# The opening of an attention and feed-forward kernel, remade: fewer warming passes, bias rows added inside PSUM, weight parts on VectorE, factor parts on ScalarE

## What is computed

```python
x = x + attn(xn, g, b, w_in, b_in, w_out, b_out) + ffn(xn, W1, b1, W2, b2)

# attn: 16 heads of 16 channels, keys are the queries
z = layernorm(xn) * g + b
q, k, v = split(z @ w_in.T + b_in);  k = q
out = softmax(q @ k.T / 4) @ v;      return out @ w_out.T + b_out
# ffn: 1024 hidden channels, weights rounded to -1, 0 or 1
h = gelu(xn @ ternary(W1).T + b1);   return h @ ternary(W2).T + b2
# ternary(w) = clip(round(w / mean(abs(w))), -1, 1)
```

## Time and profile before

| | us |
|---|---|
| median of 3 runs | 1382.27 (1381.38 to 1382.33) |
| the profiled execution, its own time | 1382.0 |
| its span on the core | 1379.8 |
| busy PE / DVE / ACT / POOL | 1359.6 / 1311.3 / 1244.9 / 230.6 |

### The profile page before, as it was taken

The page is one execution under the profiler, slowest core; times in us unless marked ns, Lnnn a source line. Parts: engine busy times, 40 slices in busy tenths (PEclk is TensorE's granted clock), DMA queues, the critical chain, the costliest instruction groups (busy, mean ns, idle before and its releaser), DMA issues.

```text
span 1379.8 us, 32101 instructions
## 1 busy us (share of the span) xinstructions
PE 1359.6 (99%) x13296; PEld 460.9 (33%) x13296; DVE 1311.3 (95%) x1350; ACT 1244.9 (90%) x2268; POOL 230.6 (17%) x385
## 2 busy tenths in 40 slices
PE   9899999999999999999999999999999999999999
PEld 6566642222222222222222222222222222222244
DVE  7888899999999999999999999999999999999935
ACT  7575569999999999999999999999999999999975
POOL 3212162000000000000000003333200225501200
PEclk9999999999999999999999999999999999999999
DMA  5333300000010001111010111000001112202122
GB/s 226 73 86 72 92 18 24 26 26 30 31 33 33 33 33 33 34 33 33 33 34 33 33 33 36 31 31 31 28 29 40 56 58 66 64 32 65 41 88 101
DMA packets 55724, 66.71 MB, mean 48 GB/s; under 512 B 33329, under 2 KB 38865, under 8 KB 55324
## 3 DMA queue, kind: packets, MB, share of 16 engines
q1 hardware_dynamic: 55146, 63.55, 14.7%
q10 hardware_dynamic: 434, 1.13, 0.2%
HBM read 40.77 MB, written 16.77 MB: 42 GB/s over the span
## 4 chain that ended last, share of the span: by engine, by line
DVE 81%; PE 15%; issue 1%; DMA 1%; ACT 1%; POOL 0%; SPq 0%; DVEq 0%
DVE part_max L988 79%; PE ps L1336 3%; PE ps L1245 3%; PE ps L1265 2%; PE ps L504 2%; PE ps L485 1%; PE ps L383 1%; PE ps L474 1%; DMA max_rows<-max_split 1%; PE ps L1358 0%; DVE w L980 0%; PE ps L514 0%; DMA x_parts<-weight_scratch 0%; PE ps L413 0%; DMA qry<-max_rows 0%
## 5 line engine op out<-in xcount | busy, mean ns | idle before, releaser
L988 DVE TENSOR_REDUCE part_max<-ps 128x1 f32<-128x1024 f32 x1024 | 1160.5, 1295 | 3.4 <-PE ps L383 3.4
L1220 ACT ACTIVATE w<-ps 128x512 f32<-128x512 f32 x2048 | 1109.4, 596 | 51.3 <-PE ps L474 16.3
L413 PE MATMUL ps<-w,v_ones 128*32 128x256 f32 (+1 forms) x7688 | 627.1, 398 | 0.3
L427 PE MATMUL ps<-qry,key 50*128 50x512 f16 x1984 | 398.9, 386 | 8.0 <-ACT w L1220 7.5
L383 PE MATMUL ps<-qry,key 48*128 48x512 f16 x2048 | 393.3, 380 | 0.7 <-DVE part_max L988 0.7
L413 PEld LDWEIGHTS ps<-w,v_ones 128*32 128x32 f32 x7688 | 151.3, 108 | 313.3 <-issue 160.2
L427 PEld LDWEIGHTS ps<-qry,key 50*128 50x128 f16 x1984 | 98.2, 92 | 430.0 <-ACT w L1220 412.3
L751 POOL COPY v_ones<-v_all 128x128 f32<-128x128 f32 x64 | 18.5, 291 | 689.0 <-PE ps L413 689.0
L383 PEld LDWEIGHTS ps<-qry,key 48*128 48x128 f16 x2048 | 100.0, 93 | 76.2 <-issue 16.0
L1336 PE MATMUL ps<-x_parts,w_ternary 128*128 128x512 f16 x256 | 62.0, 380 | 0.9 <-ACT hidden L1177 0.9
L1177 ACT ACTIVATE hidden<-ps,columns 128x512 f32<-128x512 f32 x64 | 41.2, 677 | 20.0 <-PE ps L1336 19.7
(11 more groups left out here) (169 smaller groups left out, 534.3 us busy)
## 6 DMA issues: line engine op xcount, KB each, us to landing
key<-q_parts SPq DMA_DIRECT2D x62, 128.0 KB
qry<-q_parts SPq DMA_DIRECT2D x62, 128.0 KB
o_heads<-o_evacuated SPq DMA_DIRECT2D x31, 256.0 KB, 9.9
key<-q_parts SPq DMA_DIRECT2D x66, 64.0 KB
qry<-q_parts SPq DMA_DIRECT2D x66, 64.0 KB
resid<-in_x SPq DMA_DIRECT2D x8, 512.0 KB, 7.7
q_parts<-q_split SPq DMA_DIRECT2D x16, 256.0 KB, 2.5
out<-resid SPq DMA_DIRECT2D x7, 512.0 KB, 4.0
```

Source lines behind the costliest of these rows:

```text
L413: mm = eng.matmul(pv[32 * c:32 * c + 2 * D, c0:c1], vst[:, kb, :], prob[kb % 2][:, c * BANK + c0:c * BANK + c1], start=(kb == 0), stop=(kb ...
L427: eng.matmul(ring_bank(v, i, False), key[v][r:r + KROWS, kb * P:(kb + 1) * P], qry[v][r:r + KROWS, c * BANK:(c + 1) * BANK], start=True, s ...
L988: dve.tensor_reduce(part_max[h % 2][:, blk, side:side + 1], pa[a % 2], AX.X, ALU.max).then_inc(s_r, 1)
L1220: act.activation(prob[kb % 2][:, c * BANK:(c + 1) * BANK], ring_bank(k, i, last), ACT.Exp, scale=exp_scale).then_inc(s_e, 1)
```

## The change

The lines below are from the diff, cut to its core. `WARM` falls from 16 to 10. The load of group 0's rows is cut in two, and the power -0.5 of group 0 is taken in two instructions. The replicas of the reach are made by ScalarE and not by VectorE. The absolute bias rows are a product of one row that starts each sum in PSUM, and one reduction gives both maxima. The products of `b` with the weights come behind the transposes.

```diff
-WARM = 16
+WARM = 10
 # SyncE
-            load_x(0)
+            sp.dma_start(resid[:, 0:TG // 2, :], x_v[0][:, 0:TG // 2, :]).then_inc(s_x0, 16)
+            sp.dma_start(resid[:, TG // 2:TG, :], x_v[0][:, TG // 2:TG, :]).then_inc(s_x[0], 16)
...
-            sp.wait_ge(s_sg, 8)
+            sp.wait_ge(s_sg, 6)
...
+            x_parts_in(1)
+            factors_in(1)
             store_q(0)
-            x_parts_in(1)
 # GpSimd: rsqrt(0), replicate(1), factor_rows(g)
+                    pool.tensor_tensor(rstd[:, 0, :], veps[:, 0, :], expo[:, 0, :], ALU.pow).then_inc(s_rs, 1)
+                    pool.tensor_tensor(rstd[:, 1, :], veps[:, 1, :], expo[:, 1, :], ALU.pow).then_inc(s_r0, 1)
...
                 if g == 1:
-                    pool.wait_ge(s_ft, 1)
-                else:
-                    pool.wait_ge(s_fx, 16 * (g - 1))
+                    return
+                pool.wait_ge(s_fx, 16 * (g - 1))
...
                 pool.wait_ge(s_qf, KC * g)
+                pool.wait_ge(s_xs, g)
 # VectorE: sigma in part, and its new followers
+                dve.wait_ge(s_qb, 1)
+                dve.tensor_reduce(bound[:, 0:2], pq[0].rearrange("p (s n) -> p s n", s=2), AX.X, ALU.max)
...
+            def wq_first_parts():
+                dve.wait_ge(s_wqv, 16)
+                dve.wait_ge(s_sg, 5)
+                for k in range(KC):
+                    dve.tensor_scalar(wqp[:, 0, k, :], wq[:, k, :], gq_col[:, k:k + 1], None, ALU.mult).then_inc(s_wqs, 1)
+
+            def weight_seconds(w, col, parts, first, done):
+                for k in range(KC):
+                    dve.wait_ge(first, k + 1)
+                    last = dve.scalar_tensor_tensor(out=parts[:, 1, k, :], in0=w[:, k, :], scalar=col[:, k:k + 1], in1=parts[:, 0, k, :],
+                                                    op0=ALU.mult, op1=ALU.subtract)
+                last.then_inc(done, 1)
...
 # ScalarE
+            for k in range(KC):
+                last = act.activation(reach_rep[:, k, :], ones[:, :], ACT.Identity, scale=gabs[:, k:k + 1], bias=babs[:, k:k + 1])
+            last.then_inc(s_rr, 1)
+            act.wait_ge(s_row, 16)
+            act.activation(row_abs[:, :], row[:, 0:2 * C], ACT.Abs).then_inc(s_rb, 1)
...
+            def wv_first_parts():
+                act.wait_ge(s_sg, 6)
                 for k in range(KC):
+                    act.activation(wvp[:, 0, k, :], wv[:, k, :], ACT.Identity, scale=gv_col[:, k:k + 1]).then_inc(s_wvs, 1)
+
+            def factor_parts_of_1():
+                act.wait_ge(s_fb, 2)
+                act.activation(f_rep_parts[:, 0, :, :], f_big[:, :].unsqueeze(2).to_broadcast((P, TG, P)), ACT.Copy).then_inc(s_fb, 1)
+                act.wait_ge(s_fb, 3)
+                for t in range(TG):
+                    last = act.activation(f_rep_parts[:, 1, t, :], f_rep_parts[:, 0, t, :], ACT.Identity, scale=-1.0,
+                                          bias=f_big[:, t:t + 1])
+                last.then_inc(s_fb, 1)
 # TensorE
+                    if first and o:
+                        pe.wait_ge(s_bv, 1)
...
+            pe.wait_ge(s_rr, 1)
+            pe.wait_ge(s_rb, 1)
+            for n, (out, cols) in enumerate(((bound_q, absq), (bound_v, absv))):
+                pe.matmul(out, ones[0:1, :], row_abs[:, n * C:(n + 1) * C], start=True, stop=False)
+                pe.wait_ge(s_abs, n + 2)
                 for k in range(KC):
+                    mm = pe.matmul(out, reach_rep[:, k, :], cols[:, k, :], start=False, stop=(k == KC - 1))
```

More of the change, by code:

```diff
@@ L112, in attention_ffn @@
         babs = sb("b_abs", [P, KC])
-        reach = sb("reach", [P, KC])
         reach_rep = sb("reach_rep", [P, KC, P])
@@ L846, in stats_of @@
                 x = resid[:, g * TG:(g + 1) * TG, :]
-                dve.wait_ge(s_x[g], 16)
+                if g == 0:
+                    dve.wait_ge(s_x0, 16)
+                else:
+                    dve.wait_ge(s_x[g], 16)
                 for t in range(TG):
+                    if g == 0 and t == TG // 2:
+                        dve.wait_ge(s_x[g], 16)
                     last = dve.bn_stats(stats[:, t, :], x[:, t, :])
@@ L912, in add_ffn @@
                                          op0=ALU.mult, op1=ALU.add).then_inc(s_ra, 1)
-            def reach_of_q():
-                dve.wait_ge(s_abs, 1)
-                dve.tensor_tensor(reach[:, :], gabs[:, :], babs[:, :], ALU.add).then_inc(s_sg, 1)
-                dve.wait_ge(s_sg, 1)
-                for k in range(KC):
-                    last = dve.tensor_scalar(reach_rep[:, k, :], ones[:, :], reach[:, k:k + 1], None, ALU.mult)
-                last.then_inc(s_sg, 1)
             def sigma():
@@ L933, in sigma, with other_scales @@
-                dve.tensor_reduce(bound[:, 2:3], vbound_row[:, :], AX.X, ALU.max).then_inc(s_sg, 1)
+                dve.reciprocal(inv2[:, :], floor2[:, :]).then_inc(s_sg, 1)
                 dve.wait_ge(s_sg, 4)
-                dve.tensor_scalar(bound[:, :], bound[:, :], 2.0 ** -40, 2.0 ** 60, ALU.max, ALU.min).then_inc(s_sg, 1)
+                dve.tensor_scalar(gq_col[:, :], g_col, inv2[:, 0:1], TOP, ALU.mult, ALU.mult).then_inc(s_sg, 1)
+            def other_scales():
+                dve.tensor_scalar(unsig[:, :], floor2[:, 0:1], 1.0 / TOP, None, ALU.mult)
+                dve.tensor_scalar(vun[:, :], floor2[:, 1:2], 1.0 / HTOP, None, ALU.mult)
+                dve.tensor_scalar(hu[:, :], floor2[:, 2:3], 1.0 / HTOP, None, ALU.mult)
+                dve.tensor_scalar(gv_col[:, :], g_col, inv2[:, 1:2], HTOP, ALU.mult, ALU.mult)
+                dve.tensor_scalar(vsc[:, :], inv2[:, 1:2], HTOP, None, ALU.mult)
+                dve.tensor_scalar(hs[:, :], inv2[:, 2:3], HTOP, None, ALU.mult)
@@ L1189, in _ @@
             group(0, True)
-            act.wait_ge(s_wvp, 1)
             stage_first(1)
@@ L1193, in _ @@
                 value(0, j)
+            factor_parts_of_1()
             act.wait_ge(s_ob, 1)
@@ L1286, in factor_transposes, with bias_products @@
                 mm.then_inc(s_ft, 1)
+            def bias_products():
+                for out, w in ((b_wq, wq), (b_wv, wv)):
+                    for o in range(KC):
+                        for k in range(KC):
+                            mm = pe.matmul(out[:, o:o + 1], w[:, k, o * P:(o + 1) * P], b_col[:, k:k + 1], start=(k == 0), stop=(k == KC - 1))
+                mm.then_inc(s_qb, 1)
             def group(g, between=None, early=None):
@@ L1358, in _ @@
                 pe.matmul(pf[1][:, 0:P], ones[:, :], ones[:, :], start=True, stop=True)
-            pe.wait_ge(s_row, 16)
-            pe.matmul(bank(3), ones[0:1, :], row[:, 0:2 * C], start=True, stop=True).then_inc(s_rp, 1)
             pe.wait_ge(s_abs, 1)
             pe.matmul(sum_b1, ones[:, :], b1abs[:, KF:KF + 1], start=True, stop=True)
-            pe.wait_ge(s_abs, 2)
-            pe.wait_ge(s_sg, 2)
-            for out, cols in ((bound_q, absq), (bound_v, absv)):
-                for k in range(KC):
-                    mm = pe.matmul(out, reach_rep[:, k, :], cols[:, k, :], start=(k == 0), stop=(k == KC - 1))
-            mm.then_inc(s_qb, 1)
-            for out, w in ((b_wq, wq), (b_wv, wv)):
-                for o in range(KC):
-                    for k in range(KC):
-                        mm = pe.matmul(out[:, o:o + 1], w[:, k, o * P:(o + 1) * P], b_col[:, k:k + 1], start=(k == 0), stop=(k == KC - 1))
+            pe.wait_ge(s_rr, 1)
[3 more added lines that the diff above has]
+                pe.wait_ge(s_abs, n + 2)
+                for k in range(KC):
+                    mm = pe.matmul(out, reach_rep[:, k, :], cols[:, k, :], start=False, stop=(k == KC - 1))
             mm.then_inc(s_qb, 1)
```

87 lines of the change are left out of this document (37 added, 50 removed).

## The result

| | before | after |
|---|---|---|
| median, us | 1381.41 (22 runs) | 1384.43 (22 runs) |
| lowest to highest, us | 1380.91 to 1382.34 | 1381.15 to 1392.1 |
| ratio, 95% interval | | 1.0023 (1.0015 to 1.003) |
| the profiled execution, own time and span | 1382.0, 1379.8 | 1388.76, 1386.6 |

The changed kernel is slower by 0.23%, 3.0 us, outside the range given, and its executions differ by 11 us where those of before differ by 1.4. The profiled one is among its slowest: it lies 4.3 us above the median, so the trace shows an unlucky case and not the typical one.

What follows compares the result with a forecast made beforehand. VectorE's row maxima, untouched, make 79% of the last chain; the change moves only group 1's first gelu. Transpose 3.0 us earlier, group 2's normalising 0.7 to 1.7 later, net 0.6: 1382.0 - 0.6 = 1381.4, median 1381.6; range 1379.5 to 1383.0.

Steps and rivals of the forecast that it cites:

- the price of the missing passes: Opening, TensorE: twelve bounds rows at about 0.43 us in the low clock, ending at 11.1 as before.
- The gap in q of group 0: TensorE stands 0.7 us between q's halves, waiting for the other scales and bias columns; q ends at 20.0.
- rival 1: Opening: clock already up by the bounds; gelu starts 1.6 to 2.6 us earlier, 1380.1 us; chance 0.25.
- VectorE's gain: Group 1 on VectorE: work up to the rows' transpose ends sooner, so the transpose starts 3.0 us earlier than 40.36.
- The two signs by which I would have called the forecast wrong: Groups 1 and 2: rstd of group 2 not waiting for the row sum, or line 998 keeping 1.5 us each.
- TensorE is through at 5.3 us, before the clock had come up: Opening: ten warming passes are 20 rows of 0.21 us from 1.04, ending at 5.3 us, still at the lower clock.
- rival 4: Opening through hidden blocks, TensorE: clock stays low much longer, some 4.5 us lost, 1386 us; chance 0.05.
- half loads ... act before 9 us, where the low clock sets the pace: Opening: half loads and group 0's split power cost nothing.
- a constant shift to the end: After group 1's first gelu: the program is a fixed list, so the 0.6 us shift passes through one to one.
- Rival 3: Group 1: GpSimd's power and VectorE's line 836 exclude each other; everything behind 1.3 us later, 1383.0 us; chance 0.10.
- Rival 2: Group 2: the factors are not late, so the transpose's 3.0 us gain stays, 1379.3 us; chance 0.08.

Runs made afterwards that it cites:

- e2: The changed kernel with 16 warming passes instead of 10: 1381.91 us, ratio 1.0002 to the kernel before.
- e1: The changed kernel with group 0's rows loaded by one DMA again: 1386.9 us, ratio 1.0033 to the kernel before.
- e3: The changed kernel with GpSimd's power (rstd) of group 2 ahead of the row sum of group 1: 1384.1 us, ratio 1.0016 to the kernel before.
- e5: The kernel before with only the warming cut from 16 to 10 passes: 1383.04 us, ratio 1.0014.
- e7: The changed kernel with one whole load of group 0's rows, 16 passes and group 2's power ahead of the row sum: 1378.80 us, ratio 0.9983.
- e8: The changed kernel with 16 passes and group 2's power ahead of the row sum, half loads kept: 1379.41 us, ratio 0.9991.
- e6: The changed kernel with one whole load of group 0's rows and 16 passes, GpSimd's order as changed: 1381.66 us, ratio 0.9999.
- e10: The changed kernel with one whole load and group 2's power ahead of the row sum, ten passes kept: 1381.53 us, ratio 1.0008.
- e11: e7 with the ten other-scale instructions ahead of the first ternary half of w1: 1378.64 us, ratio 0.998 to the kernel before.
- e4: The kernel before with only the load of group 0's rows cut in two: 1381.81 us, ratio 1.0004.
- e12: e8 with the load of w1 written behind ScalarE's first activation, though its issue did not move: 1380.33 us, ratio 0.9986 to the kernel before.
- e9: e8 with the ten other-scale instructions ahead of the threshold of w1: 1379.2 us, ratio 0.9986 to the kernel before.

## Why the prediction was wrong

The step that failed is the price of the missing passes. I charged the low clock for the twelve rows of the bounds alone and found that it changed nothing there. The runs show 2.5 us in the median for the six passes (e2) and a spread of 11 us, and the traces show where: a low clock that lasts past the bounds, to 14 us in e1, 18 in after and 25 in e3, and in after, e1 and e5 a second stretch of it between 45 and 57. The half loads, to which I gave no cost, add to it in the executions in which the weights land late.

**Right: how the work is strung together.** From VectorE's variance on, every step of the working is in the trace with its size, only 5 us later. Line 998 takes 4.87 (4 x 1.24 forecast) and line 905 1.22. The rows' transpose is issued at 42.33 and the row sum starts 5.7 behind it (4.7 to 5.7 forecast). The normalising of group 2 comes 8.55 behind the transpose's issue (7.6 to 8.6 forecast), and the gelu 2.45 behind that (2.56). The gap in q of group 0 is 0.83 us in e2 and e7 (0.7). Where the clock is up and the weights are early, rival 1's times hold too: in e7 the transpose is at 35.93 (35.8 forecast). That GpSimd's order, with the factors' transpose now second in SyncE's queue, takes back most of VectorE's gain is shown by e2 to e8 and e6 to e7: 2.5 and 2.9 us. The two signs by which I would have called the forecast wrong did not appear: rstd of group 2 did wait for the row sum, and line 998 ran at its clean pace. What failed was outside them.

**Wrong, first: "TensorE is through at 5.3 us, before the clock had come up", with the low clock charged up to the bounds alone.** I gave a row 0.43 us at the lower clock and 0.25 at the upper, which put the end of the bounds at 11.1 as before, and took the rest at full speed. A row costs 0.52 us at the lower level, 0.09 more than I had, and the clock does not come back when the sparse part ends: it is at 0.50 from 11 to 17 us after, and it falls again at 50 to 58. Nor did ten passes always leave the clock down: in four of the five profiles with ten passes (after, e3, e5, e10) it was up by the warming's last row or by the first rows behind it, and only in e1 was it still low when the bounds began. In after and e3 it then fell in the wait of 3.80 and 3.57 us for the late weights, in e5 behind one of 0.94, and in e10, with no such wait, it stayed up. In the kernel before the warming reaches to 7.8, past the absolute weights at 6.6 and the replicas of the reach at 7.4, and leaves no wait. That the passes are worth their time because they bridge it is my reading of these traces; no experiment separates it from their work on the clock itself. The low clock is rival 4 in kind, to which I gave 0.05 on the ground of the `KEEP` passes; they run at 20.25 after, too late for the bounds, the transposes and the `b` products. The ten passes cost 2.5, 5.2, 4.7 and 2.7 us in four pairs, and 1.6 in the kernel before (e5).

**Wrong, second: "half loads ... act before 9 us, where the low clock sets the pace", and cost nothing.** I counted the tiles they bring and not what their second issue is put ahead of. With the load in one piece the q and v weights were first read between 5.89 and 6.04 in every profile (before, e1, e5, e6, e7, e10, e11). With halves it was 5.88, 6.67, 7.08, 8.53, 9.28, 9.57 and 9.81 (e8, e2, e4, e12, e9, e3, after). A late landing moves the start and also opens a hole in TensorE, of 2.2 us in e12, 3.0 in e9, 3.6 in e3 and 3.8 in after, in or behind which the clock falls. On the median this is small, 0.3 and 0.6 us with sixteen passes, and with ten the two pairs disagree even in sign; it widens the spread (5.8 against 1.6 us, e8 and e7). In the profiled execution of after, TensorE's first product with the weights starts 3.9 us later than the 6.6 that I had. VectorE reads the bounds at 15.76 (11.1 forecast), and q of group 0 starts at 22.11 (16.5 forecast), 5.6 late. Of the gap of 0.7 between its halves less than 0.2 is left, so q ends 5.1 late (25.1, 20.0 forecast).

**Wrong, third: the place of the new hole.** I said that the emptying of the second bank is queued behind the late normalising, and charged only its lateness. It also leaves TensorE idle for 2.7 to 2.9 us (after, e1, e2, e6), and in three of these four traces (all but e2) the twelve rows behind it run at a lower clock. The forecast of "a constant shift to the end" failed with it: in the profiled execution of after the gelu is 4.8 us late, group 3 and all behind it 5.7, and the end 6.8. The last 1.0 is the longer wait for the row maxima where the heads end.

**The rivals.** Rival 3 did not happen: rstd of group 1 starts at 30.62, line 845 starts at 30.88 inside it and takes its plain 1.29, and the power ends after 1.64. The Trainium skill (SBUF — State Buffer, section "SBUF: two separate sides") says that a GpSimd instruction and a VectorE one in a two-port mode, or one with two inputs in SBUF, exclude each other on their shared ports for a whole instruction. Line 845 takes 1.29 us for as many elements as line 849, with two inputs, handles in 2.34, so I count it as of the first kind, and this pair does not show the rule; line 849 beside GpSimd's small product does (last section). My reading of the 2.92 us in the earlier trace rows, that the power's result could not be written during line 836, is not settled: in before, e4 and e5 the power took 2.92 and ended 0.04 or 0.05 us behind line 836, but in the changed kernel its plain end already lies behind line 845 (32.26 and 32.17 after). Rival 2, that the factors are not late, did not happen either. e7 makes it true by an edit and reads 1378.8, where it was priced at 1379.3, but with the clock up besides, so that the two numbers lie close is no confirmation.

**The starting point.** I subtracted from the median of three runs, 1382.27. With 22 runs the kernel before reads 1381.41, so the forecast time was 0.9 us too high from the start. (1382.27 less 0.6 is also 1381.7, and I wrote 1381.6.) As a change the forecast was 0.7 us down, and 3.0 up was measured.

**The range.** It took the spread of the runs of before, 1 us, for a kernel whose executions differ by 11. Six passes fewer remove the reserve that made every execution alike, and a median of a wide distribution lies above the execution that the steps describe.

**Open.** Why the same hole of 2.8 us lowers the clock in one execution and not in another (e6 and e2). Whether it is the distance between the issue of the q and v weights and that of `w1`, or the cut itself, that makes the landing vary: e12 did not move the issue, and an order with the weights ahead of the second half was not tried. Nor was the factors' transpose put back ahead of the rows', and what the other parts of the change are worth (bias rows in PSUM, weight parts on VectorE, factor parts on ScalarE) was not measured one by one.

**Best kernel.** e7 and e11, 1378.8 and 1378.6, are 2.7 us (0.2%) faster than before, with executions within 1.6 us of each other. The change held a gain; it needed the warming left alone and GpSimd's order changed along with SyncE's. With sixteen passes the whole load is worth 0.3 to 0.6 us in the median (e2 and e6, e8 and e7); more plainly it narrows the spread.

## What to carry to other kernels

Work that only fills (warming passes) is to be priced by all stretches that its absence could leave at the lower clock, not by the time it takes; ask also which wait it covers. A hole of 2 to 4 us in TensorE can have a second price beside its own length: it had one in after, e1, e3, e5, e6, e9 and e12, and none in before, e2 and e4. When a load is cut or a queue re-ordered, ask what now stands behind each issue and each wait, on every queue in turn: here a half load ahead of critical weights, and a power behind a row sum whose data had become late. One profile is one execution: those of after and e3 are among the slowest of their kernel and that of e10 is the fastest, and each alone would tell another story. Forecast the spread as well as the time, since a change that removes reserves shows first in how far executions lie apart.
